# Identity products on TensorE in the waits of a mixture-of-experts audio kernel

## The chip, the cores and the metric

The kernel runs on one core of a Trainium2 chip. Its time is the device time of one execution in microseconds; several executions are timed and their median is given. Before the change the median of 3 runs is 290.88 us (289.96 to 291.25).

## The reference

Sixty-four clips of 90 channels give 15 tokens each, 960 tokens in all. A token is a patch of 90 x 16 values, projected to 192 features; then come one attention layer within each clip (after a layer norm) and one mixture-of-experts layer with 16 experts, of which each token uses 4.

```python
h = einsum('bnf,ef->bne', patches, W) + b                     # 960 tokens x 192
h = h + attention(layernorm(h))                               # one head of 192, within a clip
t = rmsnorm(layernorm(h), norm_scale)
g = einsum('bth,eh->bte', t, gate_w) + gate_b                 # 16 experts
top_vals, top_idx = top_k(g, 4)
comb = scatter(softmax(top_vals), top_idx)                    # weight of each expert for each token
a = swiglu(einsum('nh,ech->nec', t, mlp1_w) + mlp1_b)         # 192 -> 768 -> 384
y = einsum('nec,ehc->neh', a, mlp2_w) + mlp2_b                # 384 -> 192
out = h + layernorm(h) + einsum('neh,ne->nh', y, comb)
```

All of it is computed in fp32, apart from the counting in the routing, which is in fp16 with whole numbers.

## The kernel before, in words

Every engine has a program of its own, written out by hand; semaphores tie them together. TensorE's program (from L883) has four stages.

*Embedding and attention* (0 to 74 us). The 960 tokens are 8 tiles of 120. `embed` (L896) makes a tile of 12 products over chunks of 120 features. The inputs of tile 0 and the embedding weights come in three pieces, of 2, 4 and 6 chunks (the table `FIRST`), each behind a semaphore of its own (`s_first`, L904); the other tiles come whole, issued by SyncE in order. After tile 0, TensorE folds the query and key weights into one product (`fold_weights`), transposes the normalised tile 0 (`turn_h`), and embeds tiles 1 and 2; then a loop over tiles interleaves embedding, attention, transposes and the gate product.

*Routing* (74 to 93 us). VectorE picks the four best experts of each token and makes one-hot masks (`hots`), first for six tiles (`EARLY`) and then for the last two; `count` (L986) sums each group's masks on TensorE. VectorE turns the counts into tiles of 128 slots per expert (45 tiles, `MT`), TensorE makes the ranks of the tokens within an expert (L1028 to L1036), and VectorE the positions (`s_pos`). Then VectorE (22) and GpSimd (10) write 32 one-hot matrices of positions, `lo_hot`; 32 products, `ps_rows` (L1067), turn these into the table of token rows per tile. Each group of four products waits for its one-hots. Meanwhile GpSimd makes the routing weights `comb`, and TensorE transposes them (L1042) and multiplies them with the second bias of all experts (`bias2`, L1048). VectorE adds the four results to the base rows (L828), after its one-hots.

*Hand-over* (91 to 102 us). When the four sums are made, SyncE issues the store of the base rows (L352) and the loads of the last four experts (`HELD`), and after these counts the experts whose weights are there (`s_ready`). TensorE's `here` (L1083) reads which expert owns a tile, waits for that count, and tells ScalarE and VectorE (`s_here`, L1090), which then stage that expert's weights. GpSimd gathers the rows of tiles 0 to 2 from HBM as soon as the table is copied, and `turn_x(0)` (L1076) transposes tile 0.

*Experts* (102 to 290 us). For each of the 45 tiles: two sets of six products of 128 x 128 with the first weights (`up`, L1098), transposes of the next tile (L1080), and three products with the second weights (`down`, L1107). GpSimd scatters the results, adding into HBM.

PSUM has 8 banks; `bank[6]` is first used by attention, `bank[2]` not between the last `turn_h` and the second `bias2`, and `bank[1]` not between the copy of the second `comb` transposes and the second `up` of tile 0.

The program's code as it stands, where the change touches it:

Of the kernel before, what the change touches and what calls it, by code (L numbers as in the profile page):

```python
# [47 lines left out]
SETTLED = 12  # L48
HELD = 4
FIRST = (0, 2, 6, FC)  # L50
EARLY = TILES - 2
POOL_EVERY = 3

def audio_tower_kernel(nc, x, tok_w, tok_b, qkv_w, qk_b, v_b, norm_scale, gate_w, gate_b,
                       w1, b1, w2, b2, out):
    ctx = ExitStack()
    with ctx:
        def sb(name, shape, dt=F32):
            return ctx.enter_context(nc.sbuf_tensor(name, shape, dt))  # L60

        def sem(name):
            return ctx.enter_context(nc.semaphore(name))
# [19 lines left out]
        ident = sb("ident", [128, 128])  # L83
# [95 lines left out]
        bank = [ctx.enter_context(nc.psum_tensor(f"bank{n}", [128, 512], F32)) for n in range(8)]  # L179
# [30 lines left out]
        s_x = [sem(f"s_x{c}") for c in range(RING)]  # L210
        s_first = [sem(f"s_first{n}") for n in range(len(FIRST) - 1)]
        s_small = sem("s_small")
# [8 lines left out]
        s_const = sem("s_const")  # L221
# [87 lines left out]
        def owners(engine, g):  # L309

            n = min(GROUP, MT - GROUP * g)
            _, found = nc.values_load_multi_w_load_instructions(
                owner[0:1, GROUP * g:GROUP * g + n], engines=[engine], min_val=0, max_val=E - 1,
                skip_runtime_bounds_check_because="owner is a count of 0 or more, held to E - 1")
            return found
# [4 lines left out]
        def _(sp):  # L320
            for n in range(len(FIRST) - 1):
                c = slice(FIRST[n], FIRST[n + 1])
                sp.dma_start(tokw_sb[:, c, :], tok_w[:, c, :]).then_inc(s_first[n], 16)
# [315 lines left out]
        def _(dve):  # L639
# [100 lines left out]
            def hots(lo, hi):  # L740

                c = slice(K * lo, K * hi)
                link(d.tensor_copy(topif[:, lo:hi, :], topi[:, lo:hi, 0:K]))
                link(d.tensor_tensor(hot3[:, c], topif[:, lo:hi, :].rearrange("p i k -> p (i k)").unsqueeze(2)
                                     .to_broadcast([TT, K * (hi - lo), E]),
                                     iota_e[:, :].unsqueeze(1).to_broadcast([TT, K * (hi - lo), E]), ALU.is_equal))
                with nc.allow_low_precision("counts of 0 and 1 are exact"):
                    d.tensor_reduce(mask[:, lo:hi, :], hot[:, lo:hi, :, :].rearrange("p i k e -> p i e k"), AX.X,
                                    ALU.add).then_inc(s_mask, 1)
# [7 lines left out]
            for i in range(TILES + 2):  # L757
# [11 lines left out]
                if i == TILES + 1:  # L769
                    dve.wait_ge(s_topi, EARLY)  # L770
                    hots(0, EARLY)
                if 2 <= i < TILES + 1:
# [14 lines left out]

            hots(EARLY, TILES)

# [94 lines left out]
        def _(pe):  # L884
            t = nc.tensor

            def turn_h(i):
                pe.wait_ge(s_hn, i + 1)
                if i >= 1:  # L890
                    pe.wait_ge(s_hTc, i)
                for c in range(HC):
                    ins = t.transpose(ps_hT[:, c, :], hn[:, i, c * HK:(c + 1) * HK], ident[0:TT, 0:TT])
                ins.then_inc(s_hT, 1)

            def embed(i):  # L896
                if i >= 1:

                    pe.wait_ge(s_x[i % RING], 16 * (i // RING + (i % RING > 0)))
                if i >= 2:  # L900
                    pe.wait_ge(s_h, i if i > 2 else 1)
                for c in range(FC):
                    if i == 0 and c in FIRST:
                        pe.wait_ge(s_first[FIRST.index(c)], 32)  # L904
                    ins = t.matmul(ps_emb[i], x_ring[:, i % RING, c, :], tokw_sb[:, c, :],  # L905
                                   start=(c == 0), stop=(c == FC - 1))
                ins.then_inc(s_emb, 1)
# [78 lines left out]
            def count(lo, hi):  # L986

                for i in range(lo, hi):
                    ins = t.matmul(ps_cnt, mask[:, i, :], ones[:, 0:TT], start=(i == 0), stop=(i == TILES - 1))
                return ins  # L990

            embed(0)
            pe.wait_ge(s_qkvw, 32)
            fold_weights()
            pe.wait_ge(s_const, 7)
            turn_h(0)
            embed(1)
            pe.wait_ge(s_small, 16 * N_SMALL)
            for i in range(TILES + 2):
                if 1 <= i <= TILES:  # L1000
                    score(i - 1)
                if i + AHEAD < TILES:
                    embed(i + AHEAD)
                if i < TILES:
                    keys(i)
                if 1 <= i <= TILES:
                    turn_p(i - 1)
                if i >= 3:
                    turn_t(i - 3)
                if i < TILES:  # L1010
                    value(i)
                if 1 <= i <= TILES:
                    context(i - 1)
                if i + 1 < TILES:
                    turn_h(i + 1)
                if i == TILES + 1:
                    turn_t(TILES - 1)
                if i >= 3:
                    gate(i - 3)
            gate(TILES - 1)  # L1020
            pe.wait_ge(s_mask, 1)
            count(0, EARLY)

            pe.wait_ge(s_mask, 2)
            count(EARLY, TILES).then_inc(s_cnt, 1)
            m2 = mask[:, :, :].rearrange("p i e -> p (i e)")
            t.matmul(ps_rank, before[:, 0:TT], m2, start=True, stop=False)  # L1028
            for s in range(1, TILES):
                t.matmul(ps_rank[:, s * E:TILES * E], ones[:, 0:TT], m2[:, 0:(TILES - s) * E],  # L1030
                         start=False, stop=False)
# [3 lines left out]
                     start=False, stop=True).then_inc(s_rank, 1)  # L1035
            t.matmul(ps_end, upto[:, :], cnt_t[:, 0:1], start=True, stop=True).then_inc(s_end, 1)  # L1036

            pe.wait_ge(s_comb, 1)
            pe.wait_ge(s_logit, TILES)
            for n in range(2):  # L1040
# [19 lines left out]
            for c in range(PAIRS):  # L1060
                if c % K == 0:

                    by_pool = (c + K) // POOL_EVERY
                    pe.wait_ge(s_hot, c + K - by_pool)
                    pe.wait_ge(s_hot_pool, by_pool)
                    pe.wait_ge(s_hi_val, c // K + 1)
                ins = t.matmul(ps_rows, lo_hot[:, c, :], hi_val[:, c, :, :],  # L1067
                               start=(c == 0), stop=(c == PAIRS - 1))
            ins.then_inc(s_rows, 1)
# [6 lines left out]
            def turn_x(j):  # L1076

                pe.wait_ge(s_got[j % GATHERS], 16 * (j // GATHERS + 1))
                for c in range(HC):
                    ins = t.transpose(ps_xT[:, c, :], xg[j % GATHERS][:, c * HK:(c + 1) * HK], ident[:, :])  # L1080
                ins.then_inc(s_xT, 1)

            def here(j):  # L1083

                if j < SETTLED:
                    pe.wait_ge(s_ready, pe.value_load(owner[0:1, j:j + 1], min_val=0, max_val=E - 1) + 1)
                if j == SETTLED:
                    pe.wait_ge(s_ready, E)
                if j <= SETTLED:
                    pe.sem_inc(s_here, 1)  # L1090
# [20 lines left out]
            pe.wait_ge(s_owner, 1)  # L1111
            here(0)
            here(1)
            pe.wait_ge(s_b2c, 1)
            turn_x(0)
            experts.extend(owners(mybir.EngineType.PE, 0))
# [61 lines left out]
```

## Time and profile before

| | |
|---|---|
| median of 3 runs | 290.88 us (289.96 to 291.25) |
| the profiled execution | 291.94 us |
| its span, first to last instruction | 290.2 us |
| mean granted clock of TensorE | 0.934 |
| TensorE products busy | 256.5 us (88%) |
| VectorE / ScalarE / GpSimd busy | 168.7 / 113.3 / 172.6 us |
| chain that ended last, by engine | TensorE 78%, DMA 9%, GpSimd 5% |

### The profile page before, as it was taken

To read this page: it belongs to the slowest core of one execution; us is meant where nothing else is said; L and a number is where in the kernel's file an instruction comes from. 1 tells how busy PE (TensorE), PEld (TensorE's weight loads), DVE (VectorE), ACT (ScalarE), POOL (GpSimd) and SP (SyncE) were. 2 spreads that over 40 slices of the span, in tenths; PEclk is the share of its full clock that TensorE was granted. 3 is DMA by queue.
4 is the path that set the end of the run, shared out by engine and by line. 5 is a ranking of instruction groups with operands and counts; after the bars stand their busy time and mean duration, and the time that the engine had idled before them with its cause. 6 is when DMAs were issued, how large, how long until landed. Compare 5 with 4: busy or idle time off the path is not lost.

```text
span 290.2 us, 6337 instructions
## 1 busy us (share of the span) xinstructions
PE 256.5 (88%) x1943; PEld 249.8 (86%) x1943; DVE 168.7 (58%) x425; ACT 113.3 (39%) x291; POOL 172.6 (59%) x202
## 2 busy tenths in 40 slices
PE   2899999997577079999999999999999999999980
PEld 1799999986456079999999999999999999999970
DVE  0014465567897117676676766767766667676640
ACT  1010212233142125545554555455455545554520
POOL 5013266668897412567776666767766666665752
PEclk9999999999655559999999999999999999999996
DMA  6998999999812993323423243422322333233100
GB/s 180 232 216 201 235 229 232 270 278 282 241 16 58 259 244 105 48 34 56 62 49 47 45 58 54 59 42 31 50 47 49 51 49 56 32 43 52 19 1 0
DMA packets 18589, 31.29 MB, mean 108 GB/s; under 512 B 5629, under 2 KB 12125, under 8 KB 18557
## 3 DMA queue, kind: packets, MB, share of 16 engines
q1 hardware_dynamic: 7862, 22.33, 31.2%
q0 software_dynamic: 8640, 7.76, 17.6%
q10 hardware_dynamic: 2055, 0.80, 1.1%
q8 instruction: 16, 0.26, 0.4%
q14 instruction: 16, 0.13, 0.1%
HBM read 26.39 MB, written 5.96 MB: 111 GB/s over the span
## 4 chain that ended last, share of the span: by engine, by line
PE 78%; DMA 9%; POOL 5%; issue 2%; DVE 2%; POOLq 1%; SPq 1%; ACT 1%; DVEq 0%
PE bank L1098 39%; PE bank L1107 14%; PE bank L905 11%; DMA hn_all<-t_rows,get_row 4%; PE bank L1080 3%; DMA x_sb<-in_x 3%; PE bank L1048 2%; PE bank L934 2%; PE bank L942 2%; DMA out<-hn_all,put_row 2%; PE bank L951 1%; POOL ln_all L429 1%; PE bank L914 1%; PE bank L1067 1%; POOL rstd L422 1%
## 5 line engine op out<-in xcount | busy, mean ns | idle before, releaser
L1098 PE MATMUL bank<-xT,x_sb 96*128 96x128 f32 (+1 forms) x1080 | 136.9, 276 | 0.8 <-ACT xT L594 0.8
L1098 PEld LDWEIGHTS bank<-xT,x_sb 96*128 96x128 f32 (+1 forms) x1080 | 131.6, 193 | 1.2 <-issue 1.2
L481 POOL DMA_INDIRECT out<-hn_all,put_row x45 | 73.0, 1622 | 52.5 <-issue 23.2
L465 POOL DMA_INDIRECT hn_all<-t_rows,get_row x45 | 47.2, 1049 | 21.0 <-issue 12.5
L1107 PE MATMUL bank<-w_sb,tokw 128*128 x270 | 51.4, 326 | 0.7 <-DVE tokw L880 0.7
L1107 PEld LDWEIGHTS bank<-w_sb,tokw 128*128 128x128 f32 x270 | 42.9, 190 | 1.0 <-issue 1.0
L869 DVE TENSOR_SCALAR ln_all<-bank 128x384 f32<-128x384 f32 x45 | 25.1, 558 | 31.4 <-PE bank L1098 31.4
L905 PE MATMUL bank<-tokw,x_sb 120*120 120x192 f32 x192 | 37.0, 353 | 6.8 <-DMA x_sb<-in_x 6.8
L611 ACT COPY x_sb<-w_sb 96x768 f32 x45 | 37.0, 823 | 12.4 <-PEq L1090 10.3
L905 PEld LDWEIGHTS bank<-tokw,x_sb 120*120 120x120 f32 x192 | 34.2, 199 | 7.8 <-DMA x_sb<-in_x 7.8
L873 DVE TENSOR_TENSOR ln_all<-ln_all 128x384 f32<-128x384 f32 x45 | 25.2, 560 | 26.5 <-ACT ln_all L630 26.5
L619 ACT ACTIVATE hn_all<-bank,weight 128x192 f32<-128x192 f32 x45 | 19.0, 421 | 49.6 <-PE bank L1107 49.6
L630 ACT ACTIVATE ln_all<-ln_all 128x384 f32<-128x384 f32 x45 | 23.5, 523 | 36.7 <-DVE ln_all L869 36.7
L858 DVE COPY x_sb<-w_sb 97x768 f32 x45 | 25.7, 573 | 6.3 <-PEq L1090 5.6
L1080 PE MATMUL bank<-ident,hn_all 128*96 128x128 f32 x90 | 17.8, 280 | 10.1 <-DMA hn_all<-t_rows,get_row 10.1
L880 DVE SCALAR_TENSOR_TENSOR tokw<-ln_all 128x384 f32<-128x384 f32 x45 | 25.2, 561 | 1.6
L875 DVE TENSOR_SCALAR ln_all<-bank 128x384 f32<-128x384 f32 x45 | 24.8, 551 | 1.2 <-PE bank L1098 1.1
L1080 PEld LDWEIGHTS bank<-ident,hn_all 128*96 128x96 f32 x90 | 10.7, 130 | 10.7 <-issue 9.8
L409 POOL TENSOR_TENSOR var_eps<-mv,eps_sb 120x1 f32<-120x1 f32 x8 | 1.8, 231 | 26.9 <-DVE mv L665 26.9
L662 DVE TENSOR_TENSOR h<-bank,tokb_sb 120x192 f32<-120x192 f32 x8 | 2.9, 358 | 25.7 <-PE bank L905 25.7
L594 ACT COPY xT<-bank 96x256 f32<-96x256 f32 x45 | 15.8, 351 | 2.7 <-PE bank L1080 2.7
L532 ACT COPY probT<-bank 120x120 f32<-120x120 f32 x8 | 2.1, 259 | 19.3 <-PE bank L959 19.3
(143 smaller groups left out, 229.4 us busy)
## 6 DMA issues: line engine op xcount, KB each, us to landing
w_sb<-in_w SPq DMA_DIRECT2D x16, 576.0 KB, 14.8
x_sb<-in_x SPq DMA_DIRECT2D x7, 675.0 KB, 10.9
w_sb<-in_w SPq DMA_DIRECT2D x16, 288.0 KB, 15.9
t_rows<-hn_all ACTq DMA_DIRECT2D x8, 90.0 KB, 7.9
out<-h SPq DMA_DIRECT2D x1, 720.0 KB, 6.1
hn_all<-t_rows,get_row POOLq DMA_INDIRECT x45, 3.2
out<-hn_all,put_row POOLq DMA_INDIRECT x45, 3.5
tokw<-in_tok_w SPq DMA_DIRECT2D x1, 540.0 KB, 6.7
```

The source lines that it names most:

```text
L465: g.indirect_dma_start(out=xg[slot], out_offset=None, in_=t_rows, in_offset=bass.IndirectOffsetOnAxis(ap=get_row[:, m:m + 1], axis=0),).th ...
L481: g.indirect_dma_start(out=out, out_offset=bass.IndirectOffsetOnAxis(ap=put_row[:, m:m + 1], axis=0), in_=ysb[m % RING], in_offset=None, c ...
L611: a.copy(stage[0:HK, j % 2, 0, :], w1_sb[0:HK, bass.ds(experts[j] * W1E, 2 * I)]).then_inc(s_stage_0, 1)
L858: d.tensor_copy(stage[:, j % 2, 1, :], w1_sb[0:HK + 1, bass.ds(experts[j] * W1E + 2 * I, 2 * I)]).then_inc(s_stage_1, 1)
L869: d.tensor_scalar(glu, ps_glu, LIMIT, None, ALU.min).then_inc(s_gluc, 1)
L873: d.tensor_tensor(gs, glu, sig, ALU.mult).then_inc(s_gs, 1)
L875: d.tensor_scalar(lin, ps_lin, LIMIT, -LIMIT, ALU.min, ALU.max).then_inc(s_linc, 1)
L880: d.scalar_tensor_tensor(out=aT[:, j % 2], in0=lin, scalar=1.0, in1=gs, op0=ALU.add, op1=ALU.mult).then_inc(s_a, 1)
L905: ins = t.matmul(ps_emb[i], x_ring[:, i % RING, c, :], tokw_sb[:, c, :], start=(c == 0), stop=(c == FC - 1))
L1080: ins = t.transpose(ps_xT[:, c, :], xg[j % GATHERS][:, c * HK:(c + 1) * HK], ident[:, :])
L1098: ins = t.matmul(dst[:, m * SLOTS:(m + 1) * SLOTS], stage[0:rows, j % 2, c, o:o + 128], xT[0:rows, j % 2, c, :], start=(c == 0), stop=(c = ...
L1107: ins = t.matmul(ps_y, aT[:, j % 2, c * SLOTS:(c + 1) * SLOTS], w2_sb[:, bass.ds(experts[j] * W2E + c * H, H)], start=(c == 0), stop=(c == ...
```

## The change

A helper multiplies the 128 x 128 identity by itself in fp32 into a PSUM bank that holds nothing at the time; nobody reads the result. TensorE now waits for the identity (`s_const`, 1) at its start, and runs 5, 5 and 9 of these products ahead of the waits for the three pieces of tile 0, 8 between the two groups of counts, 6 ahead of the transposes of `comb`, one at the head of each of the last seven groups of row products, behind that group's waits, and 14 between `here(1)` and the transposes of the first gathered tile. In all 54 products. No other instruction is moved or changed.

```diff
+FILL = (5, 5, 9)
...
+            def keep_busy(n, free):
+
+                for _ in range(n):
+                    t.matmul(free[:, 0:128], ident[:, :], ident[:, :], start=True, stop=True)
+
...
                     if i == 0 and c in FIRST:
+                        keep_busy(FILL[FIRST.index(c)], bank[6])
                         pe.wait_ge(s_first[FIRST.index(c)], 32)
...
+            pe.wait_ge(s_const, 1)
             embed(0)
...
             count(0, EARLY)
-
+            keep_busy(8, bank[2])
 
             pe.wait_ge(s_mask, 2)
             count(EARLY, TILES).then_inc(s_cnt, 1)
...
             t.matmul(ps_end, upto[:, :], cnt_t[:, 0:1], start=True, stop=True).then_inc(s_end, 1)
 
+            keep_busy(6, bank[2])
             pe.wait_ge(s_comb, 1)
...
                     pe.wait_ge(s_hi_val, c // K + 1)
+                    if c > 0:
+                        keep_busy(1, bank[1])
                 ins = t.matmul(ps_rows, lo_hot[:, c, :], hi_val[:, c, :, :],
...
             here(0)
             here(1)
+            keep_busy(14, bank[1])
             pe.wait_ge(s_b2c, 1)
             turn_x(0)
```

At the hand-over, TensorE's program read before (`owner` is the table of tile owners; L1086 is `here`, L1080 the transposes of `turn_x(0)`):

```order
L1086 TENSOR_LOAD owner [waits s_owner,s_b1]
L1086 ISA x2
L1086 REGISTER_ALU
L1086 TENSOR_LOAD owner [waits s_ready]
L1086 ISA x2
L1086 REGISTER_ALU
L1080 MATMUL bank<-ident,hn_all 96x128 [waits s_ready,s_got0,s_b2c]
```

and with the change (L1097 is `here`, L892 the helper, L1091 the transposes):

```order
L1097 TENSOR_LOAD owner [waits s_owner,s_b1]
L1097 ISA x2
L1097 REGISTER_ALU
L1097 TENSOR_LOAD owner [waits s_ready]
L1097 ISA x2
L1097 REGISTER_ALU
L892 MATMUL bank<-ident 128x128 [waits s_ready]
L892 MATMUL bank<-ident 128x128 x13
L1091 MATMUL bank<-ident,hn_all 96x128 [waits s_got0,s_b2c]
```

The 14 products stand behind both waits for `s_ready` and ahead of the wait for the gathered rows (`s_got0`).

## Rows read from the trace of the kernel before

**Rows 1.** The page's slices: granted clock of TensorE in 40 slices of 7.25 us, in tenths.
```profile
PEclk9999999999655559999999999999999999999996
```
**Rows 2.** Short windows: length, TensorE busy (records), granted clock, DMA share, GB/s.
```profile
74.10:74.30 0.20, 0.00 (x0) 0.61 0.95 323
...
108.20:108.30 0.10, 0.10 (x3) 0.61 0.45 84
```
**Rows 3.** Timeline of TensorE at the start: start, duration, line, tiles, records.
```profile
3.68 1.63 PE L905 MATMUL bank<-tokw,x_sb 120*120 120x192 f32 x4 [3.68 <-DMA x_sb<-in_x]
7.54 2.91 PE L905 MATMUL bank<-tokw,x_sb 120*120 120x192 f32 x8 [2.22 <-DMA x_sb<-in_x]
11.32 4.19 PE L905 MATMUL bank<-tokw,x_sb 120*120 120x192 f32 x12 [0.87 <-DMA x_sb<-in_x]
15.31 1.22 PE L914 MATMUL bank<-qkvw 96*96 96x193 f32 x4
...
16.65 0.87 PE L914 MATMUL bank<-qkvw 96*96 96x193 f32 x4
...
26.11 0.99 PE L934 MATMUL bank<-hT,fold 96*96 96x120 f32 x8
```
**Rows 4.** Chain of waits in order of time: a later embedding.
```profile
28.38 3.90 PE bank L905 x24
```
**Rows 5.** Timeline of TensorE, start of the expert stage.
```profile
102.38 0.63 PE L1080 MATMUL bank<-ident,hn_all 128*96 128x128 f32 x2 [9.63 <-DMA hn_all<-t_rows,get_row]
103.84 2.90 PE L1098 MATMUL bank<-xT,x_sb 96*128 96x128 f32 x12 [0.83 <-ACT xT L594]
...
106.96 3.48 PE L1098 MATMUL bank<-xT,x_sb 96*128 96x128 f32 x24
```
**Rows 6.** Timeline of TensorE in the routing.
```profile
71.15 0.32 PE L959 MATMUL bank<-ident,prob 120*120 120x120 f32 x1 [1.27 <-ACT prob L525]
...
76.49 0.77 PE L989 MATMUL bank<-ones,mask 120*16 120x120 f16 x6
78.83 0.37 PE L989 MATMUL bank<-ones,mask 120*16 120x120 f16 x2 [1.57 <-DVE mask L748]
...
82.66 1.77 PE L1042 MATMUL bank<-ident,comb 120*16 120x120 f32 x8 [1.93 <-POOL comb L457]
84.36 2.91 PE L1048 MATMUL bank<-b_sb,combT 16*120 16x192 f32 x8
...
90.17 2.58 PE L1067 MATMUL bank<-x_sb 120*128 120x90 f16 x32
```
**Rows 7.** GpSimd's identity; SyncE's issues of tiles 1 and 2; their landing after issue.
```profile
1.56 0.29 POOL L378 TENSOR_SCALAR_AFFINE_SELECT ident<-ident 128x128 f32<-128x128 f32 x1 [0.25 <-POOL ident L377]
...
6.42 0.47 SPq L336 DMA_DIRECT2D x_sb<-in_x  x1
...
x_sb<-in_x SPq DMA_DIRECT2D x1, 675.0 KB, 10.9
...
8.90 0.47 SPq L336 DMA_DIRECT2D x_sb<-in_x  x1
...
x_sb<-in_x SPq DMA_DIRECT2D x1, 675.0 KB, 12.3
```
**Rows 8.** Timeline of GpSimd, VectorE and SyncE in the routing.
```profile
82.97 7.96 POOL L461 TENSOR_SCALAR x_sb<-iota_s,qkvw 120x128 f16<-120x128 f16 x10 [0.36 <-DVE qkvw L808]
...
89.15 1.92 DVE L828 TENSOR_TENSOR h<-h,bank 120x384 f32<-120x384 f32 x4
...
91.10 0.37 SPq L352 DMA_DIRECT2D out<-h  x1
```
**Rows 9.** TensorE's sequencer in `here`: duration in ns min/median/max, first to last start.
```profile
L1090 PEldq EVENT_SEMAPHORE  x13: 51/51/51, 98.8 to 141.5; - x13
...
L1086 PEldq TENSOR_LOAD <-owner x12: 300/309/489, 91.3 to 137.7; - x12
```
**Rows 10.** Chain of waits in order of time: the first gather, issue to landing.
```profile
93.30 8.95 DMA hn_all<-t_rows,get_row
```

## The prediction

> **What bounds the kernel now.** I read three views in this order: the page's clock line, the timeline of TensorE from 0 to 16 us and from 69 to 112 us, and the chain of waits. In the steady stage, some 110 to 260 us, TensorE has no pause; the change adds nothing there, so a gain or a loss must be made earlier and be carried through. The clock line [rows 1] shows one long dip, printed between slices 13 and 18. The fine windows place it: the level goes from 2.4 to 1.2 GHz at about 74.2 us and back at about 108.2 us (a mean of 0.61 in both windows) [rows 2].
>
> There is a second slow stretch that the clock line does not print. The reader can see it in durations: in the first embedding, 8 matmul records take 2.91 us and 12 take 4.19 [rows 3], while 24 records of the same kind take 3.90 later [rows 4]. That is 0.32 us a record against 0.16, so TensorE also starts at the half level. The rows of L914 become faster soon after their start at 15.31 [rows 3]; I put the end of this stretch at 16.1 us. In both cases the level came back when TensorE had worked for 4 to 5 us without a pause: 11.32 to 16.1, and 103.84 to 108.2 [rows 3, 5]. I use 4.5 us. Not all work counts alike: from 82.66 to 92.75 TensorE is never idle, with 16-column transposes, 16-row bias products and short fp16 products, and the level stays at half [rows 6, 2]. The fills are full 128x128 fp32 products like those of the experts.
>
> **The price of one fill.** The nearest rows are the experts' 128x128 products, two records each: 12 records, so 6 products, take 2.90 us at the half level including some 0.3 of drain [rows 5], so 0.43 us each; and 24 records take 3.48 across the change of level, with half of them wholly at the full one. Full speed halves it: 0.22. The fill has the same columns, so it costs 0.43 or 0.22.
>
> **The start.** The identity is ready at 1.85 us [rows 7]. Five fills at 0.43 end at 4.1, half a microsecond after the first piece (3.68) [rows 3]; two chunks of 0.64 end at 5.4. After 4.5 us of work, at 6.4, the level is up: the next five fills end near 7.0, before the second piece at 7.54. Four chunks of 0.325 end at 8.84, nine fills at 10.8, and the third piece, there at 11.32, takes 1.95 and ends at 13.3 instead of 15.3. That is 2.0 us, but not all of it is kept. Between the first embedding and the second lie 3.0 us before (15.31, and 26.11 less two embeddings of 3.90), for the weight fold, the norm of tile 0 and its transposes; so embedding 1 could start at 16.3. Its data lands at 6.42 + 10.9 = 17.32, that of embedding 2 at 8.90 + 12.3 = 21.20 [rows 7]. Embedding 2 then ends at 25.1, against 26.11 before: **1.0 us is gained**, and the transfers take the other 1.0. TensorE is busy from there to 62, so this arrives at the routing. Bounds: 2.0 if the loads land earlier, -0.5 if the level does not come up before the third piece.
>
> **The eight fills after the early counts.** They start at about 77.1 (76.49 + 0.77, less drain) and the mask comes at 78.83 [rows 6]: a wait of 1.57 us. The level went down at 74.2, so they cost 8 x 0.43 = 3.44 and end at 80.54: the last two counts are **1.7 us late**. At the full level it would be 1.76, that is nothing. VectorE's chain hangs on these counts: expert counts, ranks, positions, one-hots, owner, bias sums. It has no pause from the ranks until 91.07 (the four sums end it, 89.15 + 1.92) [rows 8], so all 1.7 appears there. SyncE issues the store of the base rows and the held experts' loads behind those sums (91.10), and only then counts the experts that are ready; TensorE's first passing of `here` is at 98.8 [rows 9]. Hence `here(0)` passes at 98.8 - 1.0 + 1.7 = 99.5.
>
> **The six fills and the seven in the row loop.** With the level back at some 82 us (77.1 + 4.5, and a pause of 0.3 for the counts' copy), the six take 1.3 and the comb transposes start at 83.7 instead of 82.66, but at twice the speed; the bias products (two rows of 2.9 us, of which one stands there) halve and all is done near 87.6, earlier than 90.17 [rows 6]. This buys nothing: the row products need GpSimd's one-hots, ten of them in 7.96 us from 82.97 [rows 8], which the late positions move to 92.6. The last group, one fill and drain end near 93.4, 0.65 later than 92.75; with the 1.0 of the start, 0.35 earlier. The other six fills lie in the waits for one-hots. The first gather, 8.95 us [rows 10], would land near 102.0.
>
> **The fourteen fills.** They stand behind `here(1)`, some 0.6 us (one more load of 0.31 and its register work) [rows 9] behind `here(0)`: start 100.1, with the level at half again, since TensorE has done nothing for 7 us. After 4.5 us, at 104.6, 10.5 are done; 3.5 x 0.22 remain: end 105.4. The tile's rows are there at 102.0 and wait. Before, they were transposed at 102.38 [rows 5], so this start is 3.0 us late. In return all behind it runs at full speed: before, from 102.38 to the end of the third set of up products (106.96 + 3.48 = 110.44) it was 8.06 us; now 1.25 for transposes, copy and issue (1.46 less half of 0.43), three times 1.34, 0.2 for the next transposes and 0.15 of drain, 5.6 us: end 111.0. **Net 0.6 us late.** Bounds, from this stretch's own rows: the level up at the first of the 14 (3.1 us, end 103.2) gives 108.8, 1.6 early; never up gives 106.1 + 8.06 = 114.2, 3.7 late.
>
> **The sum.** -1.0 (start) + 1.7 (late counts, through VectorE and SyncE to `here`) + 2.3 (fourteen fills beyond that) - 2.4 (expert start at full speed) = +0.6. The profiled execution took 291.94 us with a span of 290.2; it lies 1.06 above the median of the three runs, 290.88, which I carry over: 291.94 + 0.6 - 1.06 = **291.5 us**. The nearest ends of both bounds give 289.3 and 294.6.
>
> **A rule against a row.** Before the level falls at 74.2, the longest pause of TensorE is 1.27 us, ahead of 71.15 [rows 6]; what is there is thin work with short pauses. The Trainium skill (TensorE: Matmul & The Clock Gate, section Why this matters for your kernels) ties a drop in mid-kernel to a long idle gap between bursts. By that rule the eight fills would meet a full clock and cost nothing; the trace does not agree, and the sum goes by the row.
>
> **Rivals.**
> - *The level still stands when the eight fills come* (faster). Thin work is not idleness, and the fall may come at another moment in another execution; against it, the fall lies 3 us ahead of the fills, and the thin stretch lasts longer than that. Price: the 1.7 is gone, `here(0)` passes at 97.8, the fourteen run from 98.4 to 103.7 (5.3, since 7 idle microseconds lie ahead of them still), and the third up set ends at 109.3, 1.1 early: 289.8 us. The rule above leads here.
> - *The level does not come back in the routing* (slower): the counts, ranks and 16-column work between the fills may not count, as from 82.66 on. Then the six cost 2.58 from about 82.4 (82.66 less its idle 1.93, plus 1.7) and the transposes start 2.3 late; the seven in the row loop cost 3.0 on the path, the rows end 5.3 later, the gather is issued at 97.6 and lands near 106.5, behind the fills. With the level up by then, +1.6; with up products at half, 106.5 + 8.06 = 114.6, +4.1. Middle: 293.7 us. It decides from the point where the comb transposes start later than 84 us at half speed.
> - *The fills do not lift the level at all*, as the identity's products may count as little as the transposes did: the start then loses 9 x 0.43 less 1.2 = 2.65 instead of gaining 1.0, the routing loses as above, and the fourteen take 6.0: about 7 us slower, 298.5.
>
> **How the numbers follow.** My forecast has 0.52, the level standing 0.23, not returning in the routing 0.19, never lifting 0.06. A change of 0.5% (1.45 us) is what a measurement here can tell from none. Faster than 289.4: a third of the first rival, and the forecast's lower tail and what I did not see (0.12): 0.20. Slower than 292.3: the last rival, most of the second (0.15), and a fifth of the forecast (0.10): 0.31. Within: 0.49. The range is the forecast's and the two nearer rivals' own: from 289.0 (level standing, with some luck in the loads) to 294.2 (second rival, upper part); it leaves out the last rival, the second's end and either tail.
>
> **What would show it.** The third embedding piece at 0.16 us a record, ending near 13.3, and the embedding of tile 2 ending near 25.1; a pause of TensorE ahead of embedding 1 that a load ends. The eight fills at 0.43 us each, and the last counts behind them 0.7 later than 78.83. `here` passing after 99, the fourteen fills partly at each speed, and transposes of tile 0 that wait for the fills instead of the gather. I am wrong if the eight fills run at 0.22, if the gather lands after the fills, or if the comb transposes stay at half.

## The result, and the profile after

The changed kernel takes 293.39 us (median of 20 runs, 290.95 to 297.85), the kernel before 291.32 us in the same comparison (20 runs, 289.40 to 295.74). The ratio of the times is 1.0059, with a 95% interval of 1.0038 to 1.0081: it is slower by 0.6%, or 1.7 us (1.1 to 2.4). Ratios here and below leave out runs more than 1.5% above the fastest of their kernel, the medians do not. The profiled execution took 292.15 us with a span of 290.4, only 0.2 us above the profiled execution before; it is one of the better ones of its kernel, and what it gives back lies after 111 us. The stage that the change is about is therefore read by places, not by the span.

The page after: the clock line that answers to [rows 1], and the group of the fills.

```profile
PE 265.9 (92%) x2051; PEld 260.0 (90%) x2051; DVE 169.0 (58%) x425; ACT 113.3 (39%) x291; POOL 172.9 (60%) x202
...
PEclk9999999999595689999999999999999999999996
...
L892 PE MATMUL bank<-ident 128*128 128x128 f32 x108 | 20.9, 354 | 7.9 <-SPq L359 6.0
```

TensorE is busier by 9.4 us, and the one long dip of the clock is now broken by a slice at full level and ends earlier; the mean granted clock went from 0.934 to 0.955. (By "level" the text means which of its two rates, 1.2 or 2.4 GHz, TensorE runs at; a "fill" is one of the added products.) By either figure the change did what it says, and the time did not follow.

The start, timeline of TensorE after (start, duration, line, tiles, records), beside [rows 3]:

```profile
1.90 2.50 PE L892 MATMUL bank<-ident 128*128 128x128 f32 x10 [1.90 <-POOL ident L379]
...
9.00 2.17 PE L892 MATMUL bank<-ident 128*128 128x128 f32 x18
11.41 2.21 PE L912 MATMUL bank<-tokw,x_sb 120*120 120x192 f32 x12 [0.24 <-DMA x_sb<-in_x]
14.05 0.89 PE L921 MATMUL bank<-qkvw 96*96 96x193 f32 x4 [0.43 <-DMA qkb_sb<-in_qk_b]
...
17.49 8.20 PE L912 MATMUL bank<-tokw,x_sb 120*120 120x192 f32 x48 [0.63 <-DMA x_sb<-in_x]
25.53 0.98 PE L941 MATMUL bank<-hT,fold 96*96 96x120 f32 x8
```

The last nine fills and the third piece run at full speed (12 records in 2.21 instead of 4.19), and the third piece ends 1.9 us earlier. Two loads then take the lead: that of the query and key bias (0.43) and that of tile 1 (0.63). The embedding of tile 2 ends at 25.53 instead of 26.11: 0.58 us kept.

The routing and the hand-over, the same view, beside [rows 6] and [rows 5]:

```profile
75.90 0.77 PE L996 MATMUL bank<-ones,mask 120*16 120x120 f16 x6
76.60 3.74 PE L892 MATMUL bank<-ident 128*128 128x128 f32 x16
80.27 0.27 PE L996 MATMUL bank<-ones,mask 120*16 120x120 f16 x2
...
82.42 1.60 PE L892 MATMUL bank<-ident 128*128 128x128 f32 x12
...
86.75 2.71 PE L1057 MATMUL bank<-b_sb,combT 16*120 16x192 f32 x8
89.40 0.48 PE L1078 MATMUL bank<-x_sb 120*128 120x90 f16 x4
89.67 0.77 PE L892 MATMUL bank<-ident 128*128 128x128 f32 x2
...
94.68 0.33 PE L1078 MATMUL bank<-x_sb 120*128 120x90 f16 x4
100.97 4.83 PE L892 MATMUL bank<-ident 128*128 128x128 f32 x28 [5.96 <-SPq L359]
105.64 0.38 PE L1091 MATMUL bank<-ident,hn_all 128*96 128x128 f32 x2
106.57 1.58 PE L1109 MATMUL bank<-xT,x_sb 96*128 96x128 f32 x12 [0.55 <-ACT xT L595]
...
108.21 3.18 PE L1109 MATMUL bank<-xT,x_sb 96*128 96x128 f32 x24
```

And the granted clock in short windows (length, then busy time and records of five engines, clock, DMA share, GB/s):

```profile
72.00:74.00 2.00, 0.62 (x5) 0.32 (x5) 1.84 (x11) 0.36 (x1) 1.22 (x5) 0.83 0.96 263
...
77.00:80.10 3.10, 3.10 (x16) 3.09 (x15) 1.59 (x6) 0.00 (x0) 3.02 (x6) 0.50 0.43 134
82.00:84.00 2.00, 1.86 (x16) 1.75 (x17) 1.58 (x5) 0.00 (x0) 0.01 (x1) 1.00 0.32 31
...
87.10:89.00 1.90, 1.90 (x8) 1.81 (x6) 1.90 (x12) 1.89 (x6) 1.90 (x4) 0.50 0.00 0
```

The eight fills run at 1.2 GHz throughout (0.50 from 77.00 to 80.10), take 3.74 us, and the last counts start at 80.27, 4.37 after the first ones; before they started 2.34 after them. The level is back for the six fills and the transposes of `comb`. It falls again in the bias products, 16 rows each, while TensorE is never idle, so five of the seven fills in the row loop are slow too, and the last row products end at 95.0 instead of 92.75.

Who is late after the counts can be followed in the timelines of GpSimd, VectorE and SyncE, beside [rows 8]: the one-hots, the base-row sums, the store of them, the first gather.

```profile
84.46 7.97 POOL L462 TENSOR_SCALAR x_sb<-iota_s,qkvw 120x128 f16<-120x128 f16 x10 [2.45 <-DVE qkvw L809]
...
90.66 1.92 DVE L829 TENSOR_TENSOR h<-h,bank 120x384 f32<-120x384 f32 x4
...
92.61 0.37 SPq L353 DMA_DIRECT2D out<-h  x1
...
95.57 1.26 POOL L466 DMA_INDIRECT hn_all<-t_rows,get_row  x1 [2.71 <-DVE get_row L833]
```

TensorE's passing of `here` (duration in ns, first to last start), beside [rows 9]:

```profile
L1101 PEldq EVENT_SEMAPHORE  x13: 51/51/51, 99.8 to 142.5; - x13
```

And the issue of the first gather, with its us to landing, from the DMA view of 95.5 to 95.8 us:

```profile
hn_all<-t_rows,get_row POOLq DMA_INDIRECT x1, 8.1
```

The positions are 1.5 us late (GpSimd starts at 84.46 instead of 82.97), the sums 1.5 (90.66 against 89.15), the store 1.5 (92.61 against 91.10), and `here` passes at 99.8 instead of 98.8. The gather lands at 95.57 + 8.1 = 103.7 and is waited for by nobody: the transposes of tile 0 follow the fourteen fills at 105.64. From the first counts to the end of the third set of up products (read at the start of the next transposes, 111.22 after, 110.27 before) the stage takes 35.32 us instead of 33.78.

### The profile page after: what moved, and what is told of

It reads as the page before. It is cut to its first block, busy times and chain, and to the rows that moved or that the text cites. A ratio compares the mean times of both kernels' runs of the same rounds, so it can differ in the third digit from the quotient of the medians.

```text
span 290.4 us, 6553 instructions
## 1 busy us (share of the span) xinstructions
PE 265.9 (92%) x2051; PEld 260.0 (90%) x2051; DVE 169.0 (58%) x425; ACT 113.3 (39%) x291; POOL 172.9 (60%) x202
## 4 chain that ended last, share of the span: by engine, by line
PE 80%; DVE 6%; SPq 4%; DMA 4%; issue 2%; POOL 1%; POOLq 1%; ACT 1%; DVEq 0%
PE bank L1109 41%; PE bank L1118 15%; PE bank L912 10%; DMA x_sb<-in_x 4%; PE bank L1091 3%; PE bank L892 3%; PE bank L941 2%; PE bank L949 2%; DVE x_sb L820 1%; PE bank L958 1%; SPq L328 1%; SPq L327 1%; PE bank L989 1%; PE bank L973 1%; DVE h L829 1%
## 5 line engine op out<-in xcount | busy, mean ns | idle before, releaser
L1109 PE MATMUL bank<-xT,x_sb 96*128 96x128 f32 (+1 forms) x1080 | 135.2, 274 | 0.6 <-ACT xT L595 0.5
L1109 PEld LDWEIGHTS bank<-xT,x_sb 96*128 96x128 f32 (+1 forms) x1080 | 129.7, 190 | 1.0 <-issue 1.0
L466 POOL DMA_INDIRECT hn_all<-t_rows,get_row x45 | 47.8, 1062 | 22.5 <-issue 13.1
L912 PE MATMUL bank<-tokw,x_sb 120*120 120x192 f32 x192 | 33.5, 331 | 1.9 <-DMA x_sb<-in_x 1.9
L912 PEld LDWEIGHTS bank<-tokw,x_sb 120*120 120x120 f32 x192 | 31.4, 186 | 2.7 <-DMA x_sb<-in_x 2.5
L892 PE MATMUL bank<-ident 128*128 128x128 f32 x108 | 20.9, 354 | 7.9 <-SPq L359 6.0
L892 PEld LDWEIGHTS bank<-ident 128*128 128x128 f32 x108 | 18.5, 257 | 8.2 <-issue 6.3
L1091 PE MATMUL bank<-ident,hn_all 128*96 128x128 f32 x90 | 17.3, 273 | 0.0
```

The lines of the kernel that those rows point to most:

```text
L466: g.indirect_dma_start(out=xg[slot], out_offset=None, in_=t_rows, in_offset=bass.IndirectOffsetOnAxis(ap=get_row[:, m:m + 1], axis=0),).th ...
L892: t.matmul(free[:, 0:128], ident[:, :], ident[:, :], start=True, stop=True)
L1109: ins = t.matmul(dst[:, m * SLOTS:(m + 1) * SLOTS], stage[0:rows, j % 2, c, o:o + 128], xT[0:rows, j % 2, c, :], start=(c == 0), stop=(c = ...
```

## The experiments

All came from the two kernels shown. "The stage" below is always this distance, from the start of the early counts to the start of tile 2's transposes, in the profiled execution: 33.78 before, 35.32 after the change. One profile gives it only roughly: in two kernels below that have no fill in this stage it took 34.41 (the start alone) and 32.94 (the start, bridged), so a difference of less than about a microsecond and a half between two profiles can be chance. The intervals are of the ratio of the time to that of the kernel before.

**The start alone.** The changed kernel with no other fills than the 19 at the start.

```diff
             count(0, EARLY)
-            keep_busy(8, bank[2])
...
-            keep_busy(6, bank[2])
             pe.wait_ge(s_comb, 1)
...
-                    if c > 0:
-                        keep_busy(1, bank[1])
...
-            keep_busy(14, bank[1])
```

> Only the 19 products of the start are left. Theory A (the cost of the change is made by the eight products after the early counts, which hold up VectorE's chain and with it SyncE's loads and the first pass of here; the start gains a little): 0.3 to 1.0 us faster than the kernel before, ratio 0.9965 to 0.999, the embedding of tile 2 ending near 25.5 instead of 26.11. Rival S (the loads of tiles 1 and 2 take all of the start's gain): ratio 1.000.

Measured: 292.70 us, ratio 1.0032 (0.9997 to 1.0068). There is no gain that can be told. Its profiled execution, the longest of its runs, has the embeddings of tiles 1 and 2 partly at the half level, and so do those of the next kernel and of the one without the six and the seven. TensorE's timeline of the next kernel (the changed kernel without the eight), whose start is the same:

```profile
16.69 9.59 PE L912 MATMUL bank<-tokw,x_sb 120*120 120x192 f32 x48 [0.59 <-DMA x_sb<-in_x]
```

and two windows of it, on either side of the embeddings' start (the clock is the third number from the end):

```profile
15.00:16.00 1.00, 1.00 (x12) 0.85 (x10) 0.38 (x1) 0.12 (x1) 0.05 (x1) 1.00 1.12 236
18.00:19.00 1.00, 1.00 (x5) 1.00 (x4) 0.00 (x0) 0.00 (x0) 0.57 (x1) 0.50 1.01 225
```

The level that the fills had bought was at full in 15 to 16 us and at half in 18 to 19; between lie one-column products, two transposes and a wait of 0.59. The 48 records take 9.59 us instead of 7.97, and embedding 2 ends at 26.11, to the hundredth where it ended before. Of the six profiled executions with these start fills, three kept the level (25.53, 25.49, 25.07) and three lost it (28.07, 26.11, 26.93). Their mean is 26.20; the six profiles below and above without start fills have a mean of 26.43 (24.93 to 29.80), so the 26.11 of the kernel before is itself only one draw.

**Without the eight.** The changed kernel, one line less.

```diff
             count(0, EARLY)
-            keep_busy(8, bank[2])
```

> The eight products after the early counts are left out, all others stay. Theory A: the last counts come about 2 us earlier than in the changed kernel, here passes first near 98.3, and the fourteen end about 1.4 us earlier; ratio to the kernel before 1.001 (0.998 to 1.003). Rival B (the fourteen cost by themselves, since they hold rows that have landed): ratio stays near 1.006. Rival C (the seven in the row loop cost, since they hold the table and the first gather): stays near 1.005.

Measured: 291.14 us, ratio 0.9988 (0.9963 to 1.0012). The interval lies wholly below that of the changed kernel; the difference of the ratios is 0.7%, 2.0 us. The last counts are back at 78.83 and `here` passes at 98.6. The stage takes 34.53 instead of 35.32, so the profile shows 0.8 of the 2.0 us, within the spread of this stage; the saving itself rests on the times. The fills behind `here` start earlier, but they take 6.02 us instead of 4.83 and so give part of it back, as TensorE's timeline shows:

```profile
78.83 0.37 PE L996 MATMUL bank<-ones,mask 120*16 120x120 f16 x2 [1.57 <-DVE mask L749]
...
99.59 6.02 PE L892 MATMUL bank<-ident 128*128 128x128 f32 x28 [6.33 <-SPq L359]
105.44 0.38 PE L1090 MATMUL bank<-ident,hn_all 128*96 128x128 f32 x2
```

**Without the fourteen.** The changed kernel, another line less.

```diff
             here(1)
-            keep_busy(14, bank[1])
             pe.wait_ge(s_b2c, 1)
```

> The fourteen products behind here(1) are left out, all others stay. Theory A: tile 0 is transposed when its rows land, near 103.7, but then all runs at the half level until some 108 us, as in the kernel before: the third set of up products ends near 112 against 111.4 in the changed kernel; ratio 1.007 (1.004 to 1.010). Rival B: the 1.9 us for which they hold landed rows come back, ratio 1.000 or less.

Measured: 293.06 us, ratio 1.0074 (1.0041 to 1.0106): no better than the changed kernel. Its profiled execution (296.54 us, well above its median, and so read for the order of things only) transposes tile 0 when the gather lands, at 103.62, and runs the first up products at the half level, the first set in 2.90 us. The timelines of GpSimd and TensorE:

```profile
95.06 1.26 POOL L466 DMA_INDIRECT hn_all<-t_rows,get_row  x1 [2.71 <-DVE get_row L833]
...
103.62 0.64 PE L1091 MATMUL bank<-ident,hn_all 128*96 128x128 f32 x2 [9.12 <-DMA hn_all<-t_rows,get_row]
```

The first gather is issued 19.20 us after the early counts start (95.06 less 75.86), where it was 16.81 before (93.30 less 76.49). So with the eight, the six and the seven in place, tile 0 is late by way of the row table and the gather, also when nothing stands behind `here`.

**Without the six and the seven.**

```diff
-            keep_busy(6, bank[2])
             pe.wait_ge(s_comb, 1)
...
                     pe.wait_ge(s_hi_val, c // K + 1)
-                    if c > 0:
-                        keep_busy(1, bank[1])
```

> The six ahead of the comb transposes and the seven in the row loop are left out, all others stay. Theory A: the row products end 1.5 to 2 us earlier than the 94.9 of the changed kernel and the first gather lands earlier, but TensorE still waits for here and for the fourteen, so the ratio stays near 1.006 (1.003 to 1.008). Rival C: the first gather sets the start of the experts, and the ratio falls to 1.000.

Measured: 293.98 us, ratio 1.0085 (1.0053 to 1.0117). This can't be told from the changed kernel. `here` passes at 101.9 in its profile and tile 0 follows the fourteen fills at 107.60, so with these in place a late row table is hidden either way.

**The fourteen alone, twice.** The kernel before with these fills only.

```diff
             here(0)
             here(1)
+            keep_busy(14, bank[1])
             pe.wait_ge(s_b2c, 1)
```

> Only the fourteen behind here(1) are left. Theory A (they delay tile 0 by what the full speed behind them gives back): start near 99.4, end near 104.7, 2.3 us after the 102.38 of the kernel before, and 2.4 us back by the third set of up products; ratio 1.000 (0.997 to 1.003). Rival B (they cost by themselves): 1.004 or more. Rival D (they are the part that gains, and the others hide it): 0.996 or less.

Measured: 296.84 us over 6 runs, ratio 1.0150 (1.0075 to 1.0226). The profiled execution had a second cause that the edit can't have: the level came back at the start only in the embeddings of tiles 1 and 2, as TensorE's timeline shows.

```profile
11.12 4.20 PE L911 MATMUL bank<-tokw,x_sb 120*120 120x192 f32 x12 [0.62 <-DMA x_sb<-in_x]
15.11 1.49 PE L920 MATMUL bank<-qkvw 96*96 96x193 f32 x4
...
16.95 1.58 PE L920 MATMUL bank<-qkvw 96*96 96x193 f32 x4
...
20.08 9.87 PE L911 MATMUL bank<-tokw,x_sb 120*120 120x192 f32 x48
```

Beside [rows 3], the second group of weight products takes 1.58 where it took 0.87, and embedding 2 ends at 29.8, 3.7 us later, ahead of anything that the fourteen touch. So it was run again.

> The kernel with only the fourteen once more. In its profiled execution the stage from the early counts to the third set of up products took 34.65 us against 33.95 in the kernel before, 0.7 more, but the first embedding's slow level lasted until 23.95 us instead of 16.1, which lies ahead of every product that was added. Theory G (its 1.5% comes from where the level returned at the start in those executions, by chance): ratio 1.001 to 1.005 now. Rival B (the fourteen by themselves cost over 1%): again 1.010 or more, with the stage still some 34.7 us.

Measured: 293.24 us, ratio 1.0054 (1.0034 to 1.0075), 1.6 us. The start was as before (25.89). The fills took 5.88 us from 99.39, tile 0 was transposed at 105.11 instead of 102.38, and the stage took 34.43 (34.49 the first time). So the fourteen behind `here` cost time by themselves. Where is not shown: tile 0 starts later, the up products behind it run faster, and the 0.65 us by which the stage is longer lies within its spread.

**The eight alone.** The kernel before with these only.

```diff
             count(0, EARLY)
+            keep_busy(8, bank[2])
```

> Only the eight between the counts are left. They end 1.7 us behind the mask, and here passes 1.7 us later, near 100.5. If theory A is right that here leads to the end by itself, ratio 1.006. If they cost only together with the fourteen, since without those TensorE waits for the gather until 102.4 and passes here(1) well before it, the gather alone is late, by some 0.5 us: ratio 1.001 to 1.003.

Measured: 291.76 us, ratio 1.0004 (0.9973 to 1.0035). No cost of theirs can be told when nothing else is added; the interval leaves room for 1.0 us. TensorE's timeline:

```profile
80.68 0.28 PE L995 MATMUL bank<-ones,mask 120*16 120x120 f16 x2
...
102.17 0.63 PE L1086 MATMUL bank<-ident,hn_all 128*96 128x128 f32 x2 [8.81 <-DMA hn_all<-t_rows,get_row]
```

The counts are as late as in the changed kernel (4.41 after the first ones), and `here` passes at 100.5, 1.7 later than before. But tile 0 waits for the gather until 102.17, so `here` has over a microsecond to spare. The gather is issued only 0.8 us later after the early counts than before (17.64 against 16.81), and tile 0 starts as soon after them as before (25.90 against 25.89). In the changed kernel the fourteen hang behind `here` and pass its lateness on to tile 0. They are not the only way: without them the rest of the changed kernel is still 0.7% slower, with the gather 2.4 us late.

**Three for eight.** The changed kernel with as many fills as the wait for the mask holds at the half level.

```diff
-            keep_busy(8, bank[2])
+            keep_busy(3, bank[2])
```

> The changed kernel with three products instead of eight between the counts: 1.3 us at the half level, inside the 1.57 us that the mask takes. Theory A: VectorE's chain is not held up, and the time falls as when all eight were left out: ratio 0.999 (0.997 to 1.002). Rival (it is not their length but the level they leave to what follows): stays near 1.006.

Measured: 291.39 us, ratio 1.0004 (0.9974 to 1.0034), below the interval of the changed kernel by a hair; 1.6 us less. The three take 1.65 us and the last counts start at 78.12, 2.34 after the first ones, as before the change. So the five fills that don't fit into the wait cost time, by the ratios about 1.6 us; in the profile the stage is 0.9 us shorter (34.42).

**The start, bridged.** Only the start fills, with two more ahead of the wait for the query and key weights and four ahead of the embedding of tile 1.

```diff
             embed(0)
+            keep_busy(2, bank[6])
             pe.wait_ge(s_qkvw, 32)
...
             turn_h(0)
+            keep_busy(4, bank[6])
             embed(1)
```

> Only the start's 19 products, and six more: two ahead of the wait for the fold's weights and four ahead of the wait for tile 1. Theory E (in the run with the start alone the clock fell again at 16.6 us, in the thin work of the weight fold and the wait for tile 1, and the embeddings of tiles 1 and 2 ran at half for 6.8 us; that takes the start's gain): the clock holds, the embedding of tile 2 ends near 25.3, ratio 0.997 (0.995 to 0.999). Rival: the start costs for another reason, ratio stays near 1.003.

Measured: 291.54 us, ratio 1.0008 (0.9966 to 1.0050). In its profile the level holds (TensorE's timeline):

```profile
16.51 1.06 PE L892 MATMUL bank<-ident 128*128 128x128 f32 x8
17.41 8.01 PE L912 MATMUL bank<-tokw,x_sb 120*120 120x192 f32 x48
25.26 0.98 PE L941 MATMUL bank<-hT,fold 96*96 96x120 f32 x8
```

The embedding ends 0.85 earlier, the early counts start at 75.63 (76.49 before), and the profiled execution took 291.25 us. In the median nothing of this is left that can be told from noise: the interval holds a gain of 1.0 and a loss of 1.5.

**Ahead of `here`, fourteen and eight.** Nothing at the start or in the routing; the fills moved into the 6 us in which TensorE waits for SyncE's count anyway.

```diff
             pe.wait_ge(s_owner, 1)
+            keep_busy(14, bank[1])
             here(0)
             here(1)
+            keep_busy(8, bank[1])
             pe.wait_ge(s_b2c, 1)
```

> None at the start and none in the routing; fourteen ahead of here(0), where TensorE waits some 6 us for SyncE, and eight behind here(1), where it waits some 3 us for the gather. Theory F (the fourteen pay for their gain only because they start at half speed in a wait that is too short for them): the level is back before 98 us, the eight take 1.8 us and end before the rows land, tile 0 is transposed near 102.4 as before but at full speed, and the third set of up products ends 2.4 us earlier: ratio 0.992 (0.990 to 0.995). Rival: the level falls again in between, or the rows land later: 0.998 to 1.002.

Measured: 291.47 us, ratio 1.0017 (0.9989 to 1.0045): missed, there is no gain. TensorE's timeline:

```profile
91.35 3.77 PE L892 MATMUL bank<-ident 128*128 128x128 f32 x28
98.66 3.42 PE L892 MATMUL bank<-ident 128*128 128x128 f32 x16 [3.53 <-SPq L359]
...
103.06 1.58 PE L1103 MATMUL bank<-xT,x_sb 96*128 96x128 f32 x12 [0.55 <-ACT xT L595]
```

and windows on the fills behind `here`:

```profile
98.70:98.90 0.20, 0.20 (x2) 0.20 (x3) 0.20 (x1) 0.20 (x1) 0.00 (x0) 1.00 0.71 191
99.20:101.00 1.80, 1.80 (x10) 1.80 (x10) 0.32 (x1) 0.08 (x1) 0.00 (x0) 0.50 0.98 219
```

The fourteen end too early. TensorE then stands still for 3.53 us, and when it goes on, the level is at full for the first records and at half from 99.2 on. That alone does not explain the miss: in this execution the first up set ran at full speed all the same, the stage took 32.40, and the whole was 1.6 us shorter than the median. Why the median shows no gain is not shown.

**Ahead of `here`, eighteen and six.** The same, with a shorter pause.

```diff
             pe.wait_ge(s_owner, 1)
+            keep_busy(18, bank[1])
             here(0)
             here(1)
+            keep_busy(6, bank[1])
             pe.wait_ge(s_b2c, 1)
```

> None at the start and in the routing; eighteen ahead of here(0) instead of fourteen, six behind here(1) instead of eight. In the run with fourteen the level came back early, they ended 3.5 us ahead of here(1), and it fell once more for 3.4 us. Theory F: with eighteen the pause is shorter, the level holds more often, and the stage from the early counts to the third up set takes 31.5 to 32.5 us instead of 33.95; ratio 0.995 (0.992 to 0.998). Rival: they overrun and hold here(0), ratio 1.000 or more.

Measured: **289.86 us, ratio 0.9963 (0.9937 to 0.9989)**: faster than the kernel before by 1.1 us (0.3 to 1.8), the only version whose whole interval lies below the kernel before. TensorE's timeline:

```profile
92.37 5.40 PE L892 MATMUL bank<-ident 128*128 128x128 f32 x36
99.33 1.58 PE L892 MATMUL bank<-ident 128*128 128x128 f32 x12 [1.55 <-SPq L359]
101.70 0.40 PE L1085 MATMUL bank<-ident,hn_all 128*96 128x128 f32 x2 [0.80 <-DMA hn_all<-t_rows,get_row]
103.15 1.57 PE L1103 MATMUL bank<-xT,x_sb 96*128 96x128 f32 x12 [1.06 <-ACT xT L595]
```

The pause ahead of `here` is 1.55 us, the level stays, the six fills end 0.8 us before the gathered rows arrive, and the first three sets of up products run at full speed. The stage takes 31.48 us, 2.3 less than before and less than in any other profile. Two cautions: this is one of a dozen versions and was measured once, and it ran on another chip than the version with fourteen and eight, each against the kernel before on its own chip.

**Both.** The bridged start and the eighteen and six.

> The start with its 19 and the six that bridge the weight fold, eighteen ahead of here(0) and six behind here(1), none in the routing. If the start's gain (0.8 us in the profiled run with the bridge) and that of the hand-over add, ratio 0.992 (0.988 to 0.996); if the level at the start falls in most executions all the same, as in g3, near 0.996.

Measured: 291.04 us, ratio 0.9981 (0.9952 to 1.0010). In its profiled execution SyncE's count came later after the fills (TensorE's timeline):

```profile
99.42 1.61 PE L892 MATMUL bank<-ident 128*128 128x128 f32 x12 [2.34 <-SPq L359]
101.84 0.64 PE L1089 MATMUL bank<-ident,hn_all 128*96 128x128 f32 x2 [0.81 <-DMA hn_all<-t_rows,get_row]
103.27 2.90 PE L1107 MATMUL bank<-xT,x_sb 96*128 96x128 f32 x12 [0.79 <-ACT xT L595]
```

A pause of 2.34 us and one of 0.81 with 1.61 of fills between them, and the first up set is back at half speed; the stage takes 33.99. So the same fills at the hand-over do not hold the level in every execution. It can't be told from the version without the bridged start, nor from no change.

## Why the prediction was right and wrong

The forecast was 291.5 us and no change that can be told (0.2% above its own profiled execution); it came 0.6% slower, inside the range, on the side that had a chance of 0.31. Step by step:

- **"The eight fills ... 1.7 us late": right.** They ran at the half level, 0.47 us each in the profile (0.43 predicted), and the last counts came 2.0 us later after the first ones than before. The path through VectorE, SyncE and `here` was right as well: `here` at 99.8 (99.5 predicted). Taken away, the changed kernel gets 2.0 us faster, cut to three 1.6. What the text did not say is the condition: "so all 1.7 appears there" holds at `here`, but alone the eight show no cost (1.0004), since tile 0 then waits for the gather. In the changed kernel the fourteen pass the lateness on; without these it comes by way of the late gather (1.0074).
- **"1.0 us is gained ... TensorE is busy from there to 62, so this arrives at the routing": wrong.** This is the term that failed. The part up to the third piece was right (its end 13.3 predicted, 13.6 seen, and the price of the fills as well), but I took the level as bought for good. Between the first embedding and the second TensorE has a thin stretch with short waits, and in three of six executions the level fell again there and the embeddings paid it back. The start alone measured 1.0032 (0.9997 to 1.0068), so a gain of 1.0 us (0.9966) is outside its interval. That what is gained arrives at the routing was right: 0.58 us at the end of the embedding of tile 2 and 0.59 at the early counts (75.90 against 76.49). With this term at nothing, the sum of the prediction is +1.6 us, and +1.7 was measured. That these agree is partly luck: the profiled execution itself was only 0.2 us longer than the one before, and the parts, measured one by one, do not add up (below).
- **"This buys nothing" (the six and the seven): not contradicted, with a mis-sized end.** The rows ended at 95.0, not 93.4 less what the start gains, since the level fell again at about 87 and four products and a fill then take 0.87 us a group. In the changed kernel this does not show, because the fourteen fills outlast the gather (landing 103.7, 102.0 predicted); with the fourteen taken away, the late rows set the start of tile 0.
- **The fourteen: right in place, uneven in size.** Predicted from 100.1 to 105.4, seen from 100.97 to 105.64, and the third up set ended at 111.4 against 111.0 predicted. Tile 0 waited for the fills instead of the gather, as forecast. Alone they were expected to pay back nearly all that they take; in three profiles without the eight in front they took 5.9 to 6.3 us instead of 5.3, as the level came back later, and alone they cost 1.6 us.
- **The rivals.** That the level still stands for the eight fills was seen in none of the four profiles that have them: the window of 72 to 74 us after the change already shows it falling (0.83; full before in that window). The Trainium skill (TensorE: Matmul & The Clock Gate, section Why this matters for your kernels) ties such a fall to a long idle gap; in the routing the trace again does not agree, and also not at 16 us without the eight, where the longest wait nearby is 0.59. At the hand-over it does: full after a pause of 1.55 us, half soon after one of 3.53; with one of 2.34 the level still stood for the fills behind it and was at half after the next 0.81. That the level does not come back in the routing was half true: it came back for the six fills and fell again in the bias products, and the fourteen hid it. That fills never lift the level was wrong from the start on: the first ten records took 2.50 us, the next ten 1.28. Its price has a slip too: about 7 us slower than the kernel before is 297.9, not 298.5.

What stays open: the parts do not add up. The start alone (+0.9) and the fourteen alone (+1.6) are slower, yet both together with the six and the seven are level with before (0.9988); the eight cost 0.7% in that company and nothing that can be told alone. Whether the six and the seven give or cost something was not tried apart, and the intervals of a microsecond each way could hold much of it.

## What to carry to other kernels

Before putting work into a wait to keep the clock up, read the clock at that very place: at the half level each fill costs twice as much, and a number that fits the wait at full speed overruns it. Put fills into waits that end with something they do not delay, ahead of the semaphore and not behind it, and let them end just before the awaited event: fourteen fills behind `here` were a loss of 1.6 us, eighteen ahead of it and six behind a gain of 1.1 us, measured once; fourteen ahead and eight behind gave nothing. A level that has been lifted can be lost again in the next thin stretch, as in three of six starts here, so a gain at one place must be followed to where the saved time is used.

## What was not expected of the hardware

The level can fall while TensorE works: in the changed kernel it fell during 16-row bias products that kept the engine busy all the time. In the kernel without the eight it fell between 16.0 and 16.6 us (a clock of 0.92 from 16.0 to 16.5, 0.50 from 16.6 to 18.0), in a wait of only 0.59 us behind one-column products and two transposes, after a stretch of some ten microseconds at full speed.

The moment of its return differs between executions of the same instructions. With no fills at the start, the third piece and the first weight group took 4.19 and 1.22 us before [rows 3], 4.20 and 1.49 with the fourteen alone; embedding 2 ended between 24.93 and 29.80 us in six such executions. The Trainium skill (TensorE: Matmul & The Clock Gate, section What's actually happening) says that the number of slow products varies from run to run; the trace agrees. Here this is a spread of several microseconds, as wide as everything that the change could win, and it is why one profile could not decide between versions that differ by one.
